# A two-layer kernel's time-mix stage: native fp32 products, mixing in PSUM, norms on ScalarE, two pairs of blocks interleaved

## The reference, cut to what matters

```python
x_prev = concatenate([x[:, :1], x[:, :-1]], axis=1)
k, v, r = split(_layernorm(x, g1, b1) @ W_tm, 3)
k = k * tmk + x_prev * (1 - tmk)          # v and r likewise with tmv, tmr
r = sigmoid(r * tmr + x_prev * (1 - tmr))
# per channel, over the 256 tokens of a sequence:
#   p = max(bb, u + k); e1 = exp(bb - p); e2 = exp(u + k - p)
#   y = (e1 * aa + e2 * v) / (e1 + e2 + 1e-8)
#   p = max(w + bb, k); e1 = exp(w + bb - p); e2 = exp(k - p)
#   aa = e1 * aa + e2 * v; bb = p + log(e1 + e2 + 1e-8)
x = x + r * y
xp = concatenate([x[:, -1:], x[:, :-1]], axis=1)
xn = _layernorm(x, g2, b2)
kk = (xn @ W_cm) * cmk4 + xp4 * (1 - cmk4)
rr = sigmoid(xn * cmr + xp * (1 - cmr))
x = x + rr * (square(relu(kk)) @ W_cp)
```

## Time and profile before

| | us |
|---|---|
| median of three runs | 842.56 |
| lowest, highest | 840.31, 845.16 |
| the profiled execution | 841.33 |
| its span, first to last instruction | 839.6 |
| PE, DVE, ACT, POOL busy | 673.5, 609.9, 419.5, 360.5 |

### The profile page before, as it was taken

The page is one execution under the profiler, slowest core; times in us unless marked ns, Lnnn a source line. Parts: engine busy times, 40 slices in busy tenths (PEclk is TensorE's granted clock), DMA queues, the critical chain, the costliest instruction groups (busy, mean ns, idle before and its releaser), DMA issues. The chain is left out here.

```text
span 839.6 us, 12507 instructions
## 1 busy us (share of the span) xinstructions
PE 673.5 (80%) x3968; PEld 511.7 (61%) x3968; DVE 609.9 (73%) x1353; ACT 419.5 (50%) x739; POOL 360.5 (43%) x421
## 2 busy tenths in 40 slices
PE   0889983136406699999999967699999997699997
...
GB/s 144 87 124 150 189 66 0 1 0 0 0 0 0 0 121 84 101 102 63 89 79 63 87 26 0 1 1 2 3 0 0 0 0 2 41 107 69 80 88 73
DMA packets 32322, 42.87 MB, mean 51 GB/s; under 512 B 5136, under 2 KB 14992, under 8 KB 32272
## 3 DMA queue, kind: packets, MB, share of 16 engines
...
## 5 line engine op out<-in xcount | busy, mean ns | idle before, releaser
L503 POOL TENSOR_TENSOR p_prod<-p_p,p_gate_row 128x512 f32<-128x512 f32 x128 | 201.8, 1585 | 139.5 <-DVE p_p L389 89.3
L303 ACT ACTIVATE p_sil<-p_ps_a 128x512 f32<-128x512 f32 x176 | 105.4, 599 | 142.3 <-PE p_ps_a L100 139.2
L394 DVE TENSOR_TENSOR p_hlo<-p_prod,p_hhi 128x512 fp32r<-128x512 f32 x176 | 150.7, 857 | 1.7 <-ACT p_hhi L312 1.4
L389 DVE TENSOR_TENSOR p_p<-p_sil,p_ps_b 128x512 f32<-128x512 f32 x128 | 87.4, 682 | 63.1 <-ACT p_sil L303 53.5
L312 ACT CAST p_hhi<-p_prod 128x512 fp32r<-128x512 f32 x176 | 108.0, 614 | 19.6 <-POOL p_prod L503 19.6
L98 PE MATMUL p_ps_acc<-p_hhi,w_downhi 128*128 128x512 f32 x176 | 71.3, 405 | 4.1 <-DVE p_hlo L394 4.0
L98 PE MATMUL p_ps_a<-xt_hi,w_uphi 128*128 128x512 f32 x176 | 74.6, 424 | 0.0
L98 PE MATMUL p_ps_b<-xt_hi,w_uphi 128*128 128x512 f32 x176 | 71.0, 403 | 0.4 <-DVE p_prod L389 0.4
L100 PE MATMUL p_ps_a<-xt_hi,w_uplo 128*128 128x512 f32 x176 | 70.3, 400 | 0.0
L100 PE MATMUL p_ps_b<-xt_hi,w_uplo 128*128 128x512 f32 x176 | 70.3, 399 | 0.0
L99 PE MATMUL p_ps_a<-xt_lo,w_uphi 128*128 128x512 f32 x176 | 70.2, 399 | 0.0
...
## 6 DMA issues: line engine op xcount, KB each, us to landing
p_gate_row<-gate_rows SPq DMA_DIRECT2D x128, 256.0 KB, 3.3
...
```

What stands on the lines that cost most here:

```text
L303: nc.scalar.activation(sil[:, u % 2], ps_a[:, u % 2], ACT.Silu).then_inc(c["sil"].sem, 1)
L389: nc.vector.tensor_tensor(dst, sil[:, u % 2], ps_b[:, u % 2], ALU.mult).then_inc(c["p1"].sem, 1)
L394: nc.vector.tensor_tensor(hlo[:, u % R], prod[:, u % R], hhi[:, u % R].bitcast(F32), ALU.subtract).then_inc(c["hlo"].sem, 1)
L503: G.tensor_tensor(prod[:, u % R], p1[:, u % 2], gate_row[:, e % ROWS], ALU.mult).then_inc(c["prod"].sem, 1)
```

## The change

The three weight matrices are kept in fp32 and multiplied as they are, one product in place of three; no high and low parts are left in this stage, and its splits in the first feed-forward stage go. Key, value and receptance are mixed with the shifted input in PSUM: `W_tm` is multiplied once by its mix row (`tmrow`, three more broadcast DMAs ahead of gate row 4), and a second product with a diagonal matrix `diag` adds the shifted input. The state is scanned by differences: `gam` is the lead of the old state over the key, its negative and positive parts (`parts`) go through the exponential, and one scan of 512 handles both sequences of a block. Both norms are applied by ACT with scale and bias by pointer (`tokens`, `tokens2`), 16 and 8 operations a pair. The other steps of the recurrence keep their operations under new names (`lead2` adds the log, `numerator` and `numerators` form and scan the numerator, `apart`, `blend`, `output`, `received`, `residual`, `wrap` lead to `x2`); `shift` and `square` are the two DVE steps of a slice, `gate_in` and `gated` the gate's. POOL keeps only the small powers, now eight tiles at once, and two more steps each for the bias. The last addition `x2 + 0.5 * tg` is done by PE: eight native products with `ident` and `half_ident` in place of four transpositions. The loop is gone: the streams are written out for four blocks, and the recurrence of blocks 2 and 3 is interleaved with the channel mix of blocks 0 and 1. `mixed` has five PSUM banks (the fifth is the receptance's, one for all blocks), `grown` three.

```diff
-    SPLIT_SLOTS = {(1, 6): 0, (1, 7): 1, (1, 8): 2, (2, 6): 3, (2, 7): 4, (3, 5): 5, (3, 6): 6, (3, 7): 7, (3, 8): 8}
+    SPLIT_SLOTS = {(2, 6): 0, (2, 7): 1, (3, 5): 2, (3, 6): 3, (3, 7): 4, (3, 8): 5}
...
+        diag, half_ident = one("diag", [P, 3, P]), one("half_ident", [P, P])
...
+        mixed = [ctx.enter_context(ps(f"rw_m{k}", [P, BLK], F32)) for k in range(5)]
+        grown = [ctx.enter_context(ps(f"rw_g{k}", [P, BLK], F32)) for k in range(3)]
...
+        def key_bank(m):
+            return mixed[2 * (m % 2)]
+        def val_bank(m):
+            return mixed[2 * (m % 2) + 1]
+        def kk_bank(n):
+            return grown[1 - n % 2]
...
+            def mix(m, q, bank):
+                h = m % 2
+                pe.matmul(bank[:], w["tm"][:, q], zf[h][:], start=True, stop=False)
+                return pe.matmul(seqs(bank[:]), diag[:, q], prev(y0[h]), start=False, stop=True)
+            def mix_key(m):
+                if m == 0:
+                    pe.wait_ge(c["r_prep"].sem, c["r_prep"].at(1))
+                pe.wait_ge(c["r_zf"].sem, c["r_zf"].at(m + 1))
+                mix(m, 0, key_bank(m)).then_inc(c["r_k"].sem, 1)
+            def mix_val(m):
+                mix(m, 1, val_bank(m)).then_inc(c["r_v"].sem, 1)
+            def mix_rec(m):
+                if m:
+                    pe.wait_ge(c["r_tr"].sem, c["r_tr"].at(m))
+                mix(m, 2, mixed[4]).then_inc(c["r_r"].sem, 1)
...
+            def grow(m, j):
+                n = GROWN * m + j
+                pe.wait_ge(c["r_zf2"].sem, c["r_zf2"].at(m + 1))
+                if n % 8 == 0:
+                    pe.wait_ge(c["r_tok2"].sem, c["r_tok2"].at(m + 2))
+                elif n % 8 == 1:
+                    pe.wait_ge(c["r_zf2"].sem, c["r_zf2"].at(m + 2))
+                else:
+                    pe.wait_ge(c["r_kx"].sem, c["r_kx"].at(n - 1))
+                pe.matmul(kk_bank(n)[:], w["cm"][:, j], zf2[m % 2][:], start=True, stop=True).then_inc(c["r_kk"].sem, 1)
+            def shrink(m, j):
+                n = GROWN * m + j
+                pe.wait_ge(c["r_sq"].sem, c["r_sq"].at(n + 1))
+                if j == 0 and m:
+                    pe.wait_ge(c["r_gate"].sem, c["r_gate"].at(m))
+                pe.matmul(grown[2][:], w["cp"][:, j], sq[n % 2][:], start=j == 0, stop=j == GROWN - 1).then_inc(c["r_vv"].sem, 1)
...
+            def turn_out(m):
+                h = m % 2
+                pe.wait_ge(c["r_gate"].sem, c["r_gate"].at(m + 1))
+                pe.wait_ge(c["r_tr"].sem, c["r_tr"].at(4))
+                if m:
+                    pe.wait_ge(c["r_out"].sem, c["r_out"].at(m))
                 for j in range(BT):
                     b, s = j // 2, j % 2
-                    last = pe.transpose((b1, b2)[h][:, bass.ts(j, P)], t4[h][:, b, s * P:(s + 1) * P], ident[:])
+                    part = mixed[4][:, bass.ts(j, P)]
+                    pe.matmul(part, x2[h][:, b, 1 + s * P:1 + (s + 1) * P], ident[:], start=True, stop=False)
+                    last = pe.matmul(part, tg[h][:, bass.ts(j, P)], half_ident[:], start=False, stop=True)
...
+            mix_val(3)
+            shrink(0, 2)
+            grow(1, 0)
+            mix_rec(3)
...
+            def tokens(m):
+                h = m % 2
+                act.wait_ge(c["r_rs"].sem, c["r_rs"].at(m // 2 + 1))
+                if m >= 2:
+                    act.wait_ge(c["r_tt"].sem, c["r_tt"].at(m - 1))
+                for dst, scale, bias in ((ytok, 1, 5), (ztok, 4, 6)):
+                    for j in range(BT):
+                        t = m * BT + j
+                        last = A(dst[h][:, j], x[:, t], ACT.Identity, bias=rs1[:, bias, t:t + 1], scale=rs1[:, scale, t:t + 1])
+                last.then_inc(c["r_tok"].sem, 1)
...
+            def logs(m):
+                h = m % 2
+                act.wait_ge(c["r_S"].sem, c["r_S"].at(m + 1))
+                A(sums[h][:, 1:1 + BLK], sums[h][:, 1:1 + BLK], ACT.Ln).then_inc(c["r_ln"].sem, 1)
...
+            def receive(m):
+                h = m % 2
                 act.wait_ge(c["r_r"].sem, c["r_r"].at(m + 1))
-                A(rg[h][:], rg[h][:], ACT.Tanh, scale=0.5).then_inc(c["r_tr"].sem, 1)
-                act.wait_ge(c["r_du"].sem, c["r_du"].at(m + 1))
-                A(t3[h][:], t3[h][:], ACT.Tanh, bias=v["nuh"], scale=0.5).then_inc(c["r_th"].sem, 1)
-            def take_ln2(h, m):
+                if m >= 2:
+                    act.wait_ge(c["r_p"].sem, c["r_p"].at(m - 1))
+                A(rg[h][:], mixed[4][:], ACT.Tanh, scale=0.5).then_inc(c["r_tr"].sem, 1)
...
+            tokens2(0)
+            tokens2(1)
+            take_in(2)
+            take_in(3)
+            take_z2(0)
+            take_z2(1)
+            receive2(0)
+            decays(2)
+            decays(3)
+            receive2(1)
+            receive(2)
+            receive(3)
+            logs(2)
+            logs(3)
...
+            def running_max(m):
+                h = m % 2
                 dve.wait_ge(c["r_k"].sem, c["r_k"].at(m + 1))
                 for b in range(NS):
-                    last = V.tensor_tensor_scan(mx[h][:, b, 1:T1], w_row(), key[h][:, b], LOW, ALU.add, ALU.max)
+                    last = V.tensor_tensor_scan(mx[h][:, b, 1:T1], v["w"].broadcast_to([P, SEQ]),
+                                                seqs(key_bank(m)[:])[:, b], LOW, ALU.add, ALU.max)
                 last.then_inc(c["r_M"].sem, 1)
-            def max_step(h, m):
+            def lead(m):
+                h = m % 2
                 dve.wait_ge(c["r_M"].sem, c["r_M"].at(m + 1))
-                V.tensor_tensor(t1[h][:], prev(mx[h]), mid(mx[h]), ALU.subtract).then_inc(c["r_dm"].sem, 1)
-            def sums(h, m):
+                if m >= 2:
+                    dve.wait_ge(c["r_th"].sem, c["r_th"].at(m - 1))
+                V.scalar_tensor_tensor(out=seqs(gam[h][:]), in0=prev(mx[h]), scalar=v["w"], in1=seqs(key_bank(m)[:]),
+                                       op0=ALU.add, op1=ALU.subtract).then_inc(c["r_g"].sem, 1)
+            def parts(m, of, done):
+                h = m % 2
+                dve.wait_ge(c[of].sem, c[of].at(m + 1))
+                V.tensor_scalar(t1[h][:], gam[h][:], 0.0, None, ALU.min)
+                V.tensor_scalar(t2[h][:], gam[h][:], 0.0, None, ALU.max).then_inc(c[done].sem, 1)
+            def total(m):
+                h = m % 2
                 dve.wait_ge(c["r_d"].sem, c["r_d"].at(m + 1))
-                for b in range(NS):
-                    last = V.tensor_tensor_scan(t3[h][:, b], t1[h][:, b], t2[h][:, b], 0.0, ALU.mult, ALU.add)
-                last.then_inc(c["r_B"].sem, 1)
-            def log_state(h, m):
+                V.tensor_tensor_scan(sums[h][:, 1:1 + BLK], t1[h][:], t2[h][:], 0.0, ALU.mult, ALU.add).then_inc(c["r_S"].sem, 1)
...
+            def lead2(m):
+                h = m % 2
                 dve.wait_ge(c["r_ln"].sem, c["r_ln"].at(m + 1))
-                V.tensor_tensor(mid(bb[h]), mid(mx[h]), t3[h][:], ALU.add).then_inc(c["r_bb"].sem, 1)
-            def peaks(h, m):
-                dve.wait_ge(c["r_bb"].sem, c["r_bb"].at(m + 1))
-                V.scalar_tensor_tensor(out=t4[h][:], in0=prev(bb[h]), scalar=v["w"], in1=key[h][:],
-                                       op0=ALU.add, op1=ALU.max).then_inc(c["r_pm"].sem, 1)
-            def peak_gap(h, m):
-                dve.wait_ge(c["r_pm"].sem, c["r_pm"].at(m + 1))
-                V.tensor_tensor(t1[h][:], prev(bb[h]), t4[h][:], ALU.subtract).then_inc(c["r_a1"].sem, 1)
-            def numerator(h, m):
+                V.tensor_tensor(gam[h][:], gam[h][:], sums[h][:, 0:BLK], ALU.add).then_inc(c["r_g2"].sem, 1)
...
+            measure2(0)
+            measure2(1)
+            moments2(0)
+            moments2(1)
+            running_max(2)
+            running_max(3)
+            lead(2)
+            lead(3)
+            gate_in(0)
+            parts(2, "r_g", "r_low")
+            gate_in(1)
+            parts(3, "r_g", "r_low")
+            shift(0)
+            shift(1)
+            square(0)
+            total(2)
+            square(1)
+            shift(2)
+            total(3)
+            square(2)
+            shift(3)
+            lead2(2)
+            square(3)
+            lead2(3)
+            shift(4)
+            parts(2, "r_g2", "r_low2")
+            parts(3, "r_g2", "r_low2")
+            square(4)
+            shift(5)
+            numerator(2)
...
+            def scale(k):
+                some = slice(2 * BT * k, 2 * BT * (k + 1))
...
+                G.tensor_tensor(r[:, 4], r[:, 3], half[:, some], ALU.pow).then_inc(c["r_c1"].sem, 1)
+                pool.wait_ge(c["r_c1"].sem, c["r_c1"].at(4 * k + 4))
+                G.tensor_tensor(r[:, 6], r[:, 4], mean, ALU.mult).then_inc(c["r_c2"].sem, 1)
+                pool.wait_ge(c["r_c2"].sem, c["r_c2"].at(k + 1))
+                G.tensor_scalar(r[:, 5:7], r[:, 5:7], -1.0, None, ALU.mult).then_inc(c["r_rs"].sem, 1)
...
```

(13 more changed lines are left out.)

724 lines of the change are left out of this document (355 added, 369 removed).

## The result

| us | before | changed |
|---|---|---|
| median | 842.3 (20 runs, 837.9 to 845.2) | 847.0 (20 runs, 841.8 to 852.9) |
| ratio, 95% interval | | 1.006 (1.0041 to 1.0079) |
| span of the profiled execution | 839.6 | 844.3 |

The changed kernel is slower by some 5 us. The forecast was 844.0 in a range of 836 to 854, and "within 0.5%" was its likeliest case; the measured 0.6% lies just on the slow side of that bound. A second set of twelve executions gave 846.6 (ratio 1.0026, 0.9997 to 1.0054). So size and range held; the side is a near miss.

The account below looks back on a forecast made before the run. DVE was taken to bound the recurrence and channel mix, hops between engines the other stretches. 841.33 - 0.5 (time-mix stage) + 1.8 (loads) = 842.6, or 843.9 on the median's footing, stated as 844; range 836 to 854.

Parts of the forecast that it names:

- within 0.5%: Whole kernel: time stays within 4.2 us of before, 838.4 to 846.8.
- to the first scan: Time-mix stage, start to first maximum scan: 19.9 us against 21.8, gain 1.9.
- recurrence of the first pair: Time-mix stage, blocks 0 and 1: less DVE work but more waits, 34.1 us against 28.3, loss 5.8.
- second norm: Time-mix stage, behind the first recurrence: 13.1 us against 10.2, loss 2.9.
- interleaved part: Second pair's recurrence with first pair's channel mix: 49.2 us against 61.4 for the same work before, gain 12.2.
- second norm, second pair: Time-mix stage, norm with nothing beside it: 11.0 us against 10.2, loss 0.8.
- last channel mix: Time-mix stage's end, blocks no longer side by side: 24.0 us against 19.9, loss 4.1.
- B: Rival, faster: pauses don't cost PE's clock, or native products cost nearer 0.54 us; 832 to 838, chance 0.24.
- C: The forecast: nothing measurable, DVE's 40 us of saved work become waits, mostly on ACT's order; chance 0.44 (with D).
- A: Rival, slower: PE becomes the bound through low clock or products at 1.07 us; 853 to 856, chance 0.32.
- feed-forward term: First feed-forward stage: three more loads ahead of block 0's gate rows 4 to 7 cost 1.8 us, bounds 1.4 and 4.
- logarithm's wait: First recurrence: DVE waits 3.9 us because `logs` stand behind `receive(1)`, which waits for `mix_rec(1)`.

Follow-up runs that it names:

- after_again: The changed kernel run once more, unaltered: 846.6 us.
- c: Changed kernel with ACT's tokens(2), tokens(3) moved behind factors(0), factors(1): 836.7 us.
- d: Changed kernel with ACT's receive(1) moved behind factors(1) and receive(3) behind factors(3): 832.4 us.
- f: Changed kernel with mix-row loads, tokens and receive moved later, plus blocks 2 and 3 turned and taken in ahead of the first pair's second norm: 812.1 us.
- j: Changed kernel without the second product of each token mix, twelve native 128x512 products fewer, part of the computation left out: 839.3 us.
- b: Kernel before, with three broadcast row loads added into a tile that nobody reads: 842.5 us.
- h: Changed kernel with 29 products that nobody reads added in PE's pauses: 836.1 us.
- g: Changed kernel with the first pair's channel mix done before the second pair's recurrence, not interleaved: 845.4 us.

## Why the prediction was right, and where it was off

| step, us | predicted | changed | after_again |
|---|---|---|---|
| start of the stage, against 127.98 | +1.8 | +4.2 | +4.3 |
| to the first scan | 19.9 | 18.4 | 18.6 |
| recurrence of the first pair | 34.1 | 34.9 | 34.7 |
| second norm | 13.1 | 13.2 | 12.9 |
| interleaved part | 49.2 | 52.4 | 51.0 |
| second norm, second pair | 11.0 | 10.5 | 10.9 |
| last channel mix | 24.0 | 24.0 | 29.1 |

**Right.** That DVE's saved work turns into waits on ACT's order, and on which: before `numerator(0)` (6.3 foreseen, 6.49), the third scan (10 and 10.43), `lead2(2)` (7.0 and 6.97); DVE busy near 82 (80.0); PE's pause in the first stage near 4.5 (4.63); the native product at 0.85 (0.86 at full clock, 1.71 at the low one). Edits *c*, *d* and *f* (`c_tokens_later` and so on) remove these waits and give 10, 15 and 15 us, so they were on the path. *B* is out by the low clock. *C*, the forecast, came out just beyond its bound of 846.8. *A* is out by its time of 853 to 856, but not by its condition, which was PE below full clock for more than a third of the 84 us from the third scan on: a mean granted clock of 0.81 over 87.2 us is the low level for 38% of them, and 0.74 over 91.3 us in `after_again` for 52%. Nor was DVE's waiting there ACT's alone: of 18.6 us idle in the interleaved part, 7.0 are behind the logarithm and 11.6 behind products. The price of *A* was too high: in *j* a product was worth less than it takes.

**The feed-forward term, +1.8, was too small.** The issue time was right (the pause grew by 1.6). The step that failed is to price a pause on PE by its length alone: behind 4.63 us the clock fell, +2. The rows had the clock low behind 3.08 us, so the warning was there. The measured +4.2 lies just outside the term's bounds of 1.4 and 4; 0.5 of it was there ahead of the pause. Against that, *b* shows that such a shift need not reach the end of the program whole.

**The first scan came 1.5 us earlier.** Some 0.9 of it is POOL's power over eight columns, for which the upper bound was taken:

```profile
135.02 1.67 POOL L1226 TENSOR_TENSOR rw_rs_all<-rw_rs_all,minus_half 128x8 f32<-128x8 f32 x1
```

1.67 and 1.64, not 2.08; two of them a pair of blocks. The other 0.6 is the key product, which took 3.08 us instead of 3.7, as the clock rose within it.

**The interleaved part was 2 to 3 us too short.** The gain of 12.2 was booked with the clock low behind two pauses of 4 us. It was low behind four, two of them of 2.1 and 2.5 us (232.18 above, and 245.35 ahead of `turn_out(1)`), and at its entrance, where the second key product came 1.72 us late. *h* gives 8 of the 52.4 us back. Rival *A*'s mechanism was at work there, at a third of its size; in `after_again` the part, the norm behind it and the last mix exceed the forecast by 6.8 us, over half of it. And the gain isn't interleaving's: *g* does without it in the same time. Nor is it the shorter recurrence's. The 61.4 us of before hold a channel mix (19.9), a recurrence (28.3) and the second pair's start (13.2); the 52.4 hold no start. On the same work the changed kernel is 4.2 us slower interleaved (52.4 against 48.2) and 6.7 slower one after the other (54.9). All the gain is the start, which is now done under the first pair's recurrence and second norm, and there cost 6.5 and 3 us until *c* and *f* moved it.

**The logarithm's wait** ahead of `lead2(0)` was 5.19, not 3.9. `mix_rec(1)`, which the tanh ahead of the logarithm waits for, ran at the low clock behind PE's 2.22 us for the receptance bank (159.65 to 163.1, 3.4 us instead of 1.7); that this is the whole difference was not tried.

**Sum.** The stage was forecast at 151.2, its measured length is 151.0, 153.7 and 157.6 in three executions of the same stage (the first with the later loads); the forecast is the fast end of what PE's clock does with it. That spread, some 3 us on average, and the feed-forward stage's 2 are the difference between 844.0 and 847.0, less 1 to 4 us that the stages behind gave back. That the sum is off by only 3 us is in part luck: terms too small by 2.4 (start), 3.2 (interleaved part) and 0.8 (first recurrence) met one too large by 1.5 (first scan) and the 1.4 from behind the stage, which nobody had forecast. Why these gave back as much (558.4 and 556.1 against 559.8) was not tried.
